# Two LayerNorm tiles instead of one per call in the attention loop of a fused attention and expert layer

## The chip, the cores and the metric

The kernel runs on the 8 cores of one Trainium2 chip. Each core works alone on half of one batch entry: 4096 tokens of 1024 channels. The cores exchange nothing. The metric is the device time in microseconds of the slowest core; lower is better.

## The reference

The layer is x + attention(LN(x)) + ffn(LN(x)). Attention covers every fourth token of a segment of 2048, so it has 512 tokens per segment, 16 heads of 64 channels and a causal mask. The feed-forward part has a shared expert and 8 routed ones (6 kept by rank), and covers all tokens.

```python
xn = _layernorm(x, axis=-1)
x = x + attn(xn, w_in, b_in, w_out, b_out) + ffn(xn, w1, w2, w3, ws1, ws2, ws3, wr)
# attn: only rows OFFSET::4 of each 2048-token segment; softmax over 512 keys, 16 heads
# ffn:  silu(x@ws1)*(x@ws2)@ws3 + sum_e w_e * (silu(x@w1[e])*(x@w2[e]))@w3[e]
```

## The kernel before, in words

A core has two segments (seg 0 and 1). A segment is split into four groups r = 0 to 3 of 512 tokens (every fourth token each), and a group into four tiles of 128 tokens. So there are 32 tiles, numbered here 0 to 31 in the order of the queue `lnq`; tiles 0 to 3 are group (0,0), 4 to 7 group (0,1), and so on. Attention is computed for r = 0 only, the feed-forward part for every group.

Each instruction is appended by `em` to a list of its engine, with the semaphore values that it waits for. The five engines work off their own lists in order, so the order of the calls below is the order on each engine.

**LayerNorm of a tile** has two steps.
- `ln_pre` (written P4 for tile 4): SyncE loads the tile into `XF` (two slots; the load waits until the normalisation two tiles earlier has read the slot). VectorE sums it (L316). ScalarE squares it (L318) and makes mean, squared mean (L322, L325). VectorE makes the variance (L328). ScalarE takes Ln and Exp (L332, L335). VectorE normalises into `xn_tm` (L338). ScalarE's square writes to the same slot of `xn_tm`, so it waits for the transposes two tiles earlier. The chain thus changes engine four times.
- `ln_tr` (written T4): TensorE transposes `xn_tm` eight times into a PSUM bank T0 or T1 (L356), VectorE copies the bank to `XN` (L365). `XN` holds two groups.

The banks T0 and T1 are taken in turn by a counter `trtile` that `ln_tr` and `attn_pair_out` share. The transposes of weight chunks use the same two banks, T0 for even and T1 for odd chunks, by a counter of their own.

**The pump.** `ln_pump` issues at most `maxtr` second steps and `maxpre` first steps, as far as two guards allow:

```python
def can_tr(i):
    if i >= len(lnq) or lnp["pre"] <= i + 1:
        return False
    seg, j = lnq[i]
    pu = prev_user[(seg, j // NQ)]
    return pu is None or pu in ffn_done
def can_pre(i):
    return i < len(lnq) and (i < 2 or lnp["tr"] >= i - 1)
...
while moved:   # T first, then P, until neither moves
    if ntr < maxtr and can_tr(lnp["tr"]): ln_tr(...)
    if npre < maxpre and can_pre(lnp["pre"]): ln_pre(...)
```

A tile is transposed only when the next one has had its first step issued; the first step runs at most two tiles ahead of the second; a group's place in `XN` must have been released by the feed-forward group that used it.

**Attention** (`attention(seg)`, L621 to L669) loops over eight head pairs hp = 0 to 7. One turn issues, in this order:
1. `attn_pair_out` of pair hp-2 (from hp = 2 on): four transposes of `OT` (L609), VectorE copies them to `OFM` (L616);
2. at hp = 4 `do_av(3)` and `v_batch(1)`, in seg 0 with four weight chunks ahead of it;
3. `qkv_pair(hp)`: in seg 0 first the weight chunks that this pair needs. A chunk is loaded into `WinNat` by GpSimd's queue, transposed on TensorE into T0 or T1 (L211) and copied by VectorE (L227); its load waits for the transposes of the chunk two earlier. Then Q (L433, L435) and K (L449, L452) on TensorE, which ScalarE copies out (L441, L457);
4. scores of key blocks 0 and 1 (L495, L498), `do_av(hp-1)` (L580, L583, then VectorE L591, L593), exps (L509, L514), scores of blocks 2 and 3 (L524, L527), exps (L539, L544), masks on VectorE (L559);
5. in seg 0 `wpump(2)`, which issues the next two items of the list of weights (two chunks at hp = 0, loads of expert weights at the later pairs);
6. `ln_pump()`, the call that is changed (L661).

The feed-forward groups call `ln_pump()` too, with its defaults of one and one. They are not touched. Attention of seg 1 has no weight chunks: all weights are in place.

Of the kernel before, what the change touches and what calls it, by code (L numbers as in the profile page):

```python
# [31 lines left out]
def build_nc():  # L32
# [20 lines left out]
    with ctx:  # L53
# [228 lines left out]
        def wpump(n=2):  # L282
            wensure(min(wptr[0] + n, len(witems)))
# [61 lines left out]
        def ln_tr(seg, j):  # L345
            r, q = j // NQ, j % NQ
            info = lninfo[(seg, j)]
            xsl = info["xsl"]
            state["trtile"] += 1
            tb = "T%d" % (state["trtile"] % 2)  # L350

            def mk_tr(xsl=xsl, tb=tb):
                def f(t):
                    ins = None
                    for ci in range(CI):
                        ins = t.transpose(bview[tb][:, ci, :],  # L356
                                          xn_tm[:, xsl, 128 * ci:128 * (ci + 1)], ident[:])
                    return ins
                return f
            ctr = em("tensor", mk_tr(), waits=[("sv", info["cxn"])] + bw(tb),  # L360
                     inc="sp")
            state["xntm_free"][xsl] = ("sp", ctr)
            rb = r % 2
            evw = [("sp", ctr)] + ([state["xnbuf_free"][rb]] if q == 0 else [])
            cev = em("vector", lambda v, rb=rb, q=q, tb=tb: v.tensor_copy(  # L365
                XN[:, rb, :, 128 * q:128 * (q + 1)], bview[tb][:, :, :]),
                waits=evw, inc="sv")
            bank[tb] = ("sv", cev)
            if q == NQ - 1:
                state["xn_ready"][(seg, r)] = cev  # L370
# [10 lines left out]
# [10 lines that stand above are left out]
        def ln_pump(maxtr=1, maxpre=1):  # L391
            ntr = npre = 0
            moved = True
            while moved:
                moved = False
                if ntr < maxtr and can_tr(lnp["tr"]):
                    ln_tr(*lnq[lnp["tr"]])
                    lnp["tr"] += 1
                    ntr += 1
                    moved = True  # L400
                if npre < maxpre and can_pre(lnp["pre"]):
                    ln_pre(*lnq[lnp["pre"]])
                    lnp["pre"] += 1
                    npre += 1
                    moved = True
# [160 lines left out]
        def av_head(seg, hp, pi, cmk):  # L566
            h = 2 * hp + pi
            obank = "Q" if pi == 0 else "K"
            ovw = oEv if pi == 0 else oOd
            vcol = 64 * h - 512 * (hp // 4)  # L570

            def mk_av(pi=pi, vcol=vcol, ovw=ovw):
                def f(t):
                    first = True
                    ins = None
                    for j in range(NQ):
                        for c in range(j + 1):
                            lt = pT[:, pi,
                                    PT_OFF[c] + 128 * (j - c):PT_OFF[c] + 128 * (j - c) + 128]
                            ins = t.matmul(ovw[:, j, 0:64], lt, Vsb[:, c, vcol:vcol + 64],  # L580
                                           start=first, stop=False)
                            first = False
                            ins = t.matmul(ovw[:, j, 64:65], lt, onescol[0:P, 0:1],  # L583
                                           start=False, stop=(j == NQ - 1 and c == j))
                    return ins
                return f
            cav = em("tensor", mk_av(),
                     waits=[("sv", cmk), state["vsb_ready"]] + bw(obank), inc="sp")
            state["pt_free"][pi] = ("sp", cav)

            crz = em("vector", lambda v, pi=pi, ovw=ovw: v.reciprocal(  # L591
                rz[:, pi, :], ovw[:, :, 64]), waits=[("sp", cav)], inc="sv")
            cno = em("vector", lambda v, pi=pi, ovw=ovw: v.tensor_tensor(  # L593
                OT[:, 0:NQ, 64 * pi:64 * pi + 64], ovw[:, :, 0:64],
                rz[:, pi, :, None].broadcast_to([P, NQ, 64]), op=ALU.mult),
                waits=[("sv", crz)] + ([state["ot_free"]] if pi == 0 else []),
                inc="sv")
            bank[obank] = ("sv", cno)
            return cno, cav

        def attn_pair_out(seg, hp, cno0, cno1):
            state["trtile"] += 1
            tb = "T%d" % (state["trtile"] % 2)

            def mk_tr(tb=tb):
                def f(t):
                    ins = None
                    for j in range(NQ):
                        ins = t.transpose(bview[tb][:, j, :], OT[:, j, :], ident[:])  # L609
                    return ins  # L610
                return f
            ctr = em("tensor", mk_tr(), waits=[("sv", cno0), ("sv", cno1)] + bw(tb),
                     inc="sp")
            state["ot_free"] = ("sp", ctr)
            evw = [("sp", ctr)] + ([state["ofm_free"]] if hp == 0 else [])
            cev = em("vector", lambda v, hp=hp, tb=tb: v.tensor_copy(  # L616
                OFM[:, hp, :], bview[tb][:, 0:NQ, :]), waits=evw, inc="sv")
            bank[tb] = ("sv", cev)
            return cev

        def attention(seg):  # L621
            pend_av = None
            pend_out = None
            last_ofm = None

            def do_av(hp, cmk_e, cmk_o):
                cne, cave = av_head(seg, hp, 0, cmk_e)
                cno, cavo = av_head(seg, hp, 1, cmk_o)
                if hp in (3, 7):
                    state["vsb_free"] = ("sp", cavo)  # L630
                    if hp == 7:
                        state["vsb_attn_done"] = ("sp", cavo)
                return cne, cno

            for hp in range(8):
                if pend_out is not None:
                    last_ofm = attn_pair_out(seg, *pend_out)
                    pend_out = None
                if hp == 4:
                    php, cmk_e, cmk_o = pend_av  # L640
                    cne, cno = do_av(php, cmk_e, cmk_o)
                    pend_out = (php, cne, cno)
                    pend_av = None
                    v_batch(seg, 1)
                eq, ek = qkv_pair(seg, hp)
                if hp == 0:
                    v_batch(seg, 0)
                cse_, cso_ = scores_c01(seg, hp, eq, ek)
                if pend_av is not None:
                    php, cmk_e, cmk_o = pend_av  # L650
                    cne, cno = do_av(php, cmk_e, cmk_o)
                    pend_out = (php, cne, cno)
                    pend_av = None
                cea, coa = exps_a(seg, hp, cse_, cso_, None)
                cse2, cso2 = scores_c23(seg, hp)
                ceb, cob = exps_b(seg, hp, cse2, cso2)
                cmk_e, cmk_o = masks(seg, hp, cea, coa, ceb, cob)
                pend_av = (hp, cmk_e, cmk_o)
                if seg == 0:
                    wpump(2)  # L660
                ln_pump()  # L661
            if pend_out is not None:
                last_ofm = attn_pair_out(seg, *pend_out)
            php, cmk_e, cmk_o = pend_av
            cne, cno = do_av(php, cmk_e, cmk_o)
            last_ofm = attn_pair_out(seg, php, cne, cno)
            state["ofm_ready"][seg] = last_ofm
# [256 lines left out]
        wensure(10)  # L924
        ensure_group(0, 0)
        attention(0)
        wensure(len(witems))
        for seg in range(NSEG):
            for r in range(NR):
                ensure_group(seg, r)  # L930
                ffn_group(seg, r)
                if seg == 0 and r == NR - 1:
                    flush_tail()
                    ensure_group(1, 0)
                    attention(1)
# [70 lines left out]
```

How the kernel before makes its waits and increments, by code:

```python
            def run(eng_obj, wt=wt, fn=fn, inc=inc, k=k):  # L139
                for s, v in wt:
                    eng_obj.wait_ge(S[s], v)
                ins = fn(eng_obj)
                if inc is not None:
                    ins.then_inc(S[inc], k)
```

## Time and profile before

| | us |
|---|---|
| two timed runs | 969.61 and 999.04, median 984.32 |
| the profiled execution, its own time | 973.35 |
| span of its slowest core (core 4), from the first to the last instruction | 971.7 |
| spans of the eight cores | 955.1 to 971.7 |
| attention of seg 0 on core 4, first Q matmul to the last transposes of `OT` | about 55 to 220 |
| attention of seg 1 on core 4 | about 554 to 665 |

The profiled execution's own time is 1.65 us more than the span of its slowest core. In the profile a line such as L338 is a line of the kernel. Busy time is summed per engine; a wait is given as "idle before, and who ended it". PE is TensorE's matmuls, DVE is VectorE, ACT is ScalarE, POOL is GpSimd and SP is SyncE.

### The profile page before, as it was taken

The page shows a single profiled execution, that of the slowest core. Times are in us where ns is not written, and L with a number is a line of the kernel's source. Part 1 is how long each engine was busy: PE and PEld are TensorE (multiplying, and loading weights), DVE is VectorE, ACT ScalarE, POOL GpSimd, SP SyncE. Part 2 cuts the span into 40 slices and gives each one's busy share as a digit, 9 for nine tenths or more (in the row PEclk, how much of TensorE's full clock was granted, in tenths as well). Part 3 has the DMA queues.
Part 4 walks back from the last instruction along what each step waited for, and adds up shares of the span by engine and source line. Part 5 has one row for each costly group of instructions (what it writes and reads, how often), then busy time and mean ns, then how long its engine had stood idle before and what let it go on. Part 6 is the DMA issues. An engine that isn't in the chain of part 4 may idle for free.

```text
span 971.7 us, 12064 instructions; the slowest of 8 cores (955.1 to 971.7 us)
## 1 busy us (share of the span) xinstructions
PE 736.2 (76%) x4126; PEld 337.5 (35%) x4192; DVE 272.2 (28%) x594; ACT 271.0 (28%) x464; POOL 94.1 (10%) x127
## 2 busy tenths in 40 slices
PE   1176646663999879958958977878999689598984
PEld 1123332333434333423423334334444233244432
DVE  3314231332330044035125024223220261232120
ACT  1223223230111163144144255332111441321111
POOL 3102021201001100200200200000002001101102
PEclk9996758675989978978979997878989799898988
DMA  5915565584003510720540630000015304502507
GB/s 100 160 45 90 84 85 69 61 136 65 1 1 76 141 45 1 168 92 1 122 116 22 129 110 22 1 2 1 1 25 117 112 8 82 136 0 42 133 3 171
DMA packets 48842, 67.40 MB, mean 69 GB/s; under 512 B 20880, under 2 KB 22928, under 8 KB 48784
## 3 DMA queue, kind: packets, MB, share of 16 engines
q0 software_dynamic: 34960, 33.06, 24.6%
q1 hardware_dynamic: 13824, 33.56, 10.3%
q8 instruction: 37, 0.61, 0.3%
q14 instruction: 21, 0.17, 0.1%
HBM read 66.11 MB, written 16.78 MB: 85 GB/s over the span
## 4 chain that ended last, share of the span: by engine, by line
PE 57%; DMA 16%; ACT 10%; DVE 8%; issue 8%; DVEq 0%; POOL 0%; ACTq 0%; SPq 0%; POOLq 0%
PE pA L821 10%; PE pB L821 8%; PE pK L874 6%; PE pQ L874 6%; PE pA L433 5%; PE pA L742 5%; DMA WinNat<-x 4%; DMA XF<-x 4%; PE pA L449 3%; PE pB L742 3%; DMA out<-osb 2%; PE ptT L211 2%; DVE st_s L316 2%; DMA WinNat<-w_in 2%; DMA osb<-x 2%
## 5 line engine op out<-in xcount | busy, mean ns | idle before, releaser
L821 PE MATMUL pA<-XN,W 128*128 128x512 bf16 x497 | 125.5, 407 | 57.2 <-ACT s1e L835 56.1
L821 PE MATMUL pB<-XN,W 128*128 128x512 bf16 x501 | 114.3, 379 | 0.6
L821 PEld LDWEIGHTS pA<-XN,W 128*128 128x128 bf16 x512 | 51.1, 103 | 123.1 <-issue 76.1
L897 POOL DMA_DIRECT2D osb<-x x32 | 27.2, 850 | 615.3 <-ACT osb L892 612.4
L211 PE MATMUL ptT<-ident,WinNat 128*128 128x128 bf16 x256 | 29.8, 299 | 66.0 <-DMA WinNat<-w_in 25.9
L821 PEld LDWEIGHTS pB<-XN,W 128*128 128x128 bf16 x512 | 50.1, 98 | 60.4
L874 PE MATMUL pQ<-W,HP 128*128 128x512 bf16 x252 | 63.7, 395 | 0.2
L874 PE MATMUL pK<-W,HP 128*128 128x512 bf16 x254 | 60.4, 379 | 0.2
L835 ACT ACTIVATE s1e<-pA 128x1024 bf16<-128x1024 f32 x32 | 32.7, 1023 | 85.3 <-PE pA L821 85.1
L316 DVE TENSOR_REDUCE st_s<-XF 128x1 f32<-128x1024 f32 x32 | 38.8, 1212 | 57.2 <-DMA XF<-x 57.2
L318 ACT ACTIVATE xn_tm<-XF 128x1024 bf16<-128x1024 f32 x32 | 33.7, 1052 | 74.5 <-DMA XF<-x 64.7
L433 PE MATMUL pA<-XN,Wqk 128*128 128x512 bf16 x116 | 44.3, 549 | 8.2 <-DVE Wqk L227 5.4
L211 PEld LDWEIGHTS ptT<-ident,WinNat 128*128 128x128 bf16 x256 | 24.3, 136 | 70.9 <-issue 70.9
L559 DVE TENSOR_TENSOR pT<-pT,utri 128x128 bf16<-128x128 bf16 x128 | 20.2, 221 | 94.7 <-ACT pT L539 93.0
L839 DVE TENSOR_TENSOR HP<-s1e,pB 128x1024 bf16<-128x1024 bf16 x32 | 39.0, 1218 | 27.7 <-PE pB L821 19.2
L742 PE MATMUL pA<-XN,Ws 128*128 128x512 bf16 x120 | 44.2, 544 | 1.5 <-issue 0.7
L804 DVE TENSOR_TENSOR HP<-HP,pQ 128x512 bf16<-128x512 bf16 x32 | 22.0, 688 | 80.7 <-PE pQ L796 79.3
L785 DVE COPY gT<-pQ 8x512 bf16<-8x512 bf16 x8 | 3.3, 410 | 141.9 <-PE pQ L779 141.9
L356 PE MATMUL ptT<-ident,xn_tm 128*128 128x128 bf16 x256 | 23.5, 245 | 21.6 <-DVE xn_tm L338 21.6
L338 DVE TENSOR_SCALAR xn_tm<-XF,st_m,st_r 128x1024 bf16<-128x1024 f32 x32 | 26.0, 813 | 45.9 <-ACT st_r L335 45.9
L874 PEld LDWEIGHTS pQ<-W,HP 128*128 128x128 bf16 x256 | 25.8, 101 | 32.8 <-issue 4.5
L874 PEld LDWEIGHTS pK<-W,HP 128*128 128x128 bf16 x256 | 25.0, 98 | 30.5 <-issue 0.6
(146 smaller groups left out, 923.8 us busy)
## 6 DMA issues: line engine op xcount, KB each, us to landing
XF<-x SPq DMA_DIRECT2D x32, 512.0 KB, 4.5
osb<-x POOLq DMA_DIRECT2D x32, 256.0 KB, 4.5
out<-osb SPq DMA_DIRECT2D x32, 256.0 KB, 4.8
WinNat<-x POOLq DMA_DIRECT2D x32, 256.0 KB, 5.4
out<-WinNat SPq DMA_DIRECT2D x32, 256.0 KB, 3.2
WinNat<-w_in POOLq DMA_DIRECT2D x24, 256.0 KB, 4.9
W<-w POOLq DMA_DIRECT2D x16, 256.0 KB, 6.7
W<-w POOLq DMA_DIRECT2D x1, 2048.0 KB, 19.7
```

What stands on the lines that cost most here:

```text
L211: ins = t.transpose(bview[tb][:, ci, :], WinNat[:, sl, 128 * ci:128 * (ci + 1)], ident[:])
L316: crs = em("vector", lambda v, seg=seg, j=j, gslot=gslot: v.reduce_sum(st_s[:, seg, j:j + 1], XF[:, gslot, :], axis=AX), waits=ldw, inc="sv")
L318: csq = em("scalar", lambda s, seg=seg, j=j, gslot=gslot, xsl=xsl: s.activation(out=xn_tm[:, xsl, :], in_=XF[:, gslot, :], func=AF.Square, ...
L338: cxn = em("vector", lambda v, seg=seg, j=j, gslot=gslot, xsl=xsl: v.tensor_scalar(out=xn_tm[:, xsl, :], in0=XF[:, gslot, :], scalar1=st_m ...
L433: t.matmul(pA[:, 0, :], Wqk[:, ci, 128 * hp:128 * (hp + 1)], XN[:, 0, ci, :], start=(ci == 0), stop=False)
L449: t.matmul(pA[:, 1, :], Wqk[:, ci, 1024 + 128 * hp:1024 + 128 * (hp + 1)], XN[:, 0, ci, :], start=(ci == 0), stop=False)
L742: ins = t.matmul(bview[bn], Wsx[:, ci, 128 * k:128 * (k + 1)], XN[:, rb, ci, :], start=(ci == 0), stop=(ci == CI - 1))
L821: ins = t.matmul(bview[bn], Wx[:, e, ci, :], XN[:, rb, ci, :], start=(ci == 0), stop=(ci == CI - 1))
L835: cse = em("scalar", lambda s: s.activation(out=s1e[:, :, :], in_=pA[:, :, :], func=AF.Silu), waits=[("sp", cw10), ("sp", cw11), last_chp2 ...
L839: cu = em("vector", lambda v, e0=e0: v.tensor_tensor(HP[:, e0:e0 + 2, :], s1e[:, :, :], pB[:, :, :], op=ALU.mult), waits=[("sa", cse), ("s ...
L874: ins = t.matmul(bview[bn], lt, rh, start=(i == 0), stop=(i == len(ops) - 1))
L897: em("gpsimd", lambda g, seg=seg, r=r, q=q, Hh=Hh, dst=dst: g.dma_start(out=dst, in_=xv[seg, r, q][:, 512 * Hh:512 * (Hh + 1)], accum_op=A ...
```

## The change

The call at the end of a turn of the attention loop may issue up to two second steps and two first steps:

```diff
@@ -658,7 +658,7 @@
                 pend_av = (hp, cmk_e, cmk_o)
                 if seg == 0:
                     wpump(2)
-                ln_pump()
+                ln_pump(maxtr=2, maxpre=2)
             if pend_out is not None:
                 last_ofm = attn_pair_out(seg, *pend_out)
             php, cmk_e, cmk_o = pend_av
```

## Rows read from the trace of the kernel before

**Rows 1.** The page's busy times and granted TensorE clock over 40 slices.

```profile
PE 736.2 (76%) x4126; PEld 337.5 (35%) x4192; DVE 272.2 (28%) x594; ACT 271.0 (28%) x464; POOL 94.1 (10%) x127
...
PEclk9996758675989978978979997878989799898988
```

**Rows 2.** Waits of TensorE, 50 to 240 us: us in total, times, longest.

```profile
PE ptT L211 <- DVE OFM L616: 21.4, 6, 5.6
```

**Rows 3.** VectorE, timeline, seg 0 around the end of hp=0.

```profile
75.82 1.21 DVE L316 TENSOR_REDUCE st_s<-XF 128x1 f32<-128x1024 f32 x1
78.58 0.81 DVE L338 TENSOR_SCALAR xn_tm<-XF,st_m,st_r 128x1024 bf16<-128x1024 f32 x1 [0.70 <-ACT st_r L335]
84.78 0.18 DVE L591 RECIPROCAL rz<-pQ 128x4 f32<-128x4 f32 x1 [5.39 <-PE pQ L583]
```

**Rows 4.** TensorE, timeline, seg 0: Q of hp=1.

```profile
75.77 3.57 PE L433 MATMUL pA<-XN,Wqk 128*128 128x512 bf16 x8 [1.22 <-DVE Wqk L227]
```

**Rows 5.** VectorE, timeline, end of hp=1: P and T ahead of OFM.

```profile
88.59 1.21 DVE L316 TENSOR_REDUCE st_s<-XF 128x1 f32<-128x1024 f32 x1
...
92.68 0.41 DVE L616 COPY OFM<-ptT 128x512 bf16<-128x512 bf16 x1
```

**Rows 6.** VectorE, timeline, ends of hp=4, hp=5 and hp=6 in seg 0.

```profile
166.00 1.22 DVE L316 TENSOR_REDUCE st_s<-XF 128x1 f32<-128x1024 f32 x1
...
170.38 0.41 DVE L616 COPY OFM<-ptT 128x512 bf16<-128x512 bf16 x1
...
185.37 1.21 DVE L316 TENSOR_REDUCE st_s<-XF 128x1 f32<-128x1024 f32 x1
...
188.86 0.42 DVE L616 COPY OFM<-ptT 128x512 bf16<-128x512 bf16 x1
...
202.50 0.42 DVE L616 COPY OFM<-ptT 128x512 bf16<-128x512 bf16 x1
```

**Rows 7.** TensorE, timeline, seg 0: weight chunks after hp=3, hp=5, hp=6.

```profile
131.28 1.87 PE L211 MATMUL ptT<-ident,WinNat 128*128 128x128 bf16 x16 [3.10 <-DVE rz L591]
...
189.43 1.01 PE L211 MATMUL ptT<-ident,WinNat 128*128 128x128 bf16 x8 [4.07 <-DVE OFM L616]
...
203.06 1.86 PE L211 MATMUL ptT<-ident,WinNat 128*128 128x128 bf16 x16 [1.44 <-DVE OFM L616]
205.72 0.63 PE L433 MATMUL pA<-XN,Wqk 128*128 128x512 bf16 x1 [0.79 <-DVE Wqk L227]
```

**Rows 8.** VectorE, timeline, seg 1, end of hp=0.

```profile
573.46 1.21 DVE L316 TENSOR_REDUCE st_s<-XF 128x1 f32<-128x1024 f32 x1
...
576.22 0.81 DVE L338 TENSOR_SCALAR xn_tm<-XF,st_m,st_r 128x1024 bf16<-128x1024 f32 x1 [0.70 <-ACT st_r L335]
580.13 0.18 DVE L591 RECIPROCAL rz<-pQ 128x4 f32<-128x4 f32 x1 [3.10 <-PE pQ L583]
```

**Rows 9.** ScalarE, timeline, seg 1: Q and K copied out, hp=1 and hp=2.

```profile
576.02 0.58 ACT L441 ACTIVATE Q<-pA 128x512 bf16<-128x512 f32 x1
577.88 0.60 ACT L457 ACTIVATE K<-pA 128x512 bf16<-128x512 f32 x1 [1.28 <-PE pA L452]
...
587.11 0.58 ACT L441 ACTIVATE Q<-pA 128x512 bf16<-128x512 f32 x1
589.23 0.60 ACT L457 ACTIVATE K<-pA 128x512 bf16<-128x512 f32 x1 [1.54 <-PE pA L452]
```

**Rows 10.** TensorE, timeline, seg 1: a turn end with LayerNorm (593) and one without (637).

```profile
593.59 0.37 PE L524 MATMUL pB<-Q,K 64*128 64x256 bf16 x1 [0.44 <-ACT pT L514]
...
595.67 3.19 PE L433 MATMUL pA<-XN,Wqk 128*128 128x512 bf16 x7 [0.22 <-issue]
...
637.04 0.37 PE L524 MATMUL pB<-Q,K 64*128 64x256 bf16 x1 [0.59 <-ACT pT L514]
...
638.27 1.06 PE L433 MATMUL pA<-XN,Wqk 128*128 128x512 bf16 x2 [0.22 <-ACT pT L544]
```

**Rows 11.** Loads of a LayerNorm tile, all 32.

```profile
DMA to landing us min/median/max: 3.3/4.5/10.9
```

## The prediction, made before the changed kernel ran

> **What bounds the kernel now.** I read the page first. TensorE is busy 76% of the span, VectorE and ScalarE 28% each [rows 1]. So the end is set by TensorE and by what TensorE waits for, and the question for this change is where LayerNorm stands in TensorE's way. The granted clock says where TensorE is thin: its digits are lowest in the 4th to 9th slice of 24 us, which is attention of segment 0.
>
> Then the waits of TensorE in that stretch. The largest is for weight chunks, six times, 21.4 us in all, and it is ended by VectorE's copy of `OFM` [rows 2]. A chunk's transposes need bank T0 or T1, the bank is freed by that copy, and the copy stands on VectorE behind the LayerNorm step that the pump issued at the end of the turn before. The timelines show it: at the end of hp=1 the tile's reduction starts at 88.59 and `OFM` follows at 92.68, 4.09 us later [rows 5]. At hp=5, where only a P is issued, it is 188.86 - 185.37 = 3.49 us, and at hp=6, without LayerNorm, the chunks wait only 1.44 us [rows 6, 7]. So in segment 0 each tile's chain of engine changes lies bare on the path. In segment 1 there are no chunks, Q and K of the next pair do not wait for VectorE, and the same chain lies beside them: ScalarE takes Q out at 576.02, just after the chain's last step [rows 8, 9].
>
> **What the change issues.** The calls follow from the guards. Segment 0 enters attention with tiles 0 to 3 done. Before: hp=0 P4; hp=1 P5 T4; hp=2 P6 T5; hp=3 P7 T6; hp=4 P8 T7; hp=5 P9; then tile 8 is held back, as its place in `XN` is in use. After: hp=0 P4 P5 T4; hp=1 P6 T5 P7 T6; hp=2 P8 T7 P9; nothing later. Segment 1 enters with T19 and P21 done. Before: hp=0 to 3 one pair each (T20 P22 to T23 P25). After: hp=0 T20 P22 T21 P23; hp=1 T22 P24 T23 P25; nothing later. Both ways leave attention with the same tiles done (T7, P9 and T23, P25), so every feed-forward call is what it was. No instruction is added or removed; ten steps of work move two or three pairs earlier. They lay one to a turn and now lie two to a turn.
>
> **Segment 0, turn by turn.**
> - End of hp=0: P4 cost nothing before. It ran on VectorE while TensorE did Q and K of hp=1, and VectorE was idle for 5.39 us before the next `rz` [rows 3]. P5 (3.49 us) fits there. But T4 is now issued on TensorE ahead of Q of hp=1 and waits for P4's normalisation, which ends at 78.58 + 0.81 = 79.39. Eight transposes take 1.01 us (the same shape at L211 [rows 7]), so Q starts at about 80.4 in place of 75.77 [rows 4]: **+4.6**. Behind T4 on TensorE stand Q, K, the scores and AV of the pair, and all wait with it. This is the one new wait.
> - End of hp=1: one P and T become two, in series on VectorE, all ahead of `OFM`: **+4.1** [rows 5]. T6 on TensorE waits for P6, but P7 holds `OFM` longer.
> - End of hp=2: P8 T7 P9 in place of P6 T5: one P more, **+3.5** [rows 6].
> - End of hp=3: P7 T6 are gone. `trtile` now gives `OT`'s transposes the other bank, so the first chunk no longer needs `OFM` at all; it needs the AV matmuls to be out of the way. TensorE's idle time ahead of it, 3.10 us, goes: **-3.1** [rows 7].
> - End of hp=4: P8 T7 gone, reduction 166.00 to `OFM` 170.38: **-4.4** [rows 6].
> - End of hp=5: P9 gone: **-3.5** [rows 6]. Next late there, as at hp=6, is the wait from the masks over `OFM` to the chunks [rows 7].
>
> Sum: 12.2 given, 11.0 got back, **+1.2**. What was serial stays serial; the change loses because T4 stands in front of its own first step and gains nothing for it. The bounds of the T4 term: 0 if Q of hp=1 had been as late anyway, 4.6 as worked out; the row of Q at 75.77 says that it was not late, so I take 4.6.
>
> **Segment 1.** Here ScalarE's order decides. Q's copy is issued behind the whole chain of the pump. Before, it started 576.02 - 573.46 = 2.56 us after the reduction [rows 8, 9], and Q's last matmul was just done. With a second P behind the first (and T21's copy between), the second reduction starts 4.09 us after the first, at 577.55, and Q's copy at 580.1; K's follows 0.6 us later, at 580.7, against 577.88: **+2.8**. The scores of hp=1 wait for K, and exps, masks and the pair's end behind them. VectorE's own 3.10 us of idle time ahead of `rz` [rows 8] hides nearly all of its part, since AV moves too. At hp=2 the same: Q at 587.11 + 4.09 = 591.2, K at 591.8 against 589.23: **+2.6**. In return the turn ends of hp=2 and hp=3 lose their transposes. From the last score matmuls to Q it is 595.67 - 593.59 = 2.08 us with LayerNorm and 638.27 - 637.04 = 1.23 us without [rows 10]: **-0.9** at hp=2. At hp=3 AV waits for the masks anyway; I take half of it, **-0.5**. Sum: **+4.0**. Bounds: below, 1.4 us less than nothing, if ScalarE's copies were not held up at all; above 5.4, if nothing came back.
>
> Both together: 973.35 + 1.2 + 4.0 = **978.5 us**, against the profiled execution. The two runs shown lie at 969.61 and 999.04; the profiled one is near the lower, and the median of the two, 984.32, is not a time that any run had. A change of +0.5% is well within the 2% that a measurement of this kernel can about tell from no change.
>
> **The clock.** Waits grow at three turns and shrink at three. In segment 0 the Q matmuls run at the low level, 1.2 GHz, after long waits and short ones: 3.57 us for eight after 1.22 us of idle time [rows 4], 0.63 us for the first one of hp=7 after 0.79 us, with 1.44 us before the chunks [rows 7]. So I count no change. The Trainium skill says (TensorE: Matmul & The Clock Gate, section "Why this matters for your kernels") that idle gaps between bursts of matmuls put the array back to half its clock. By that rule doubling three waits costs and the shortened ones pay; the trace agrees that matmuls after a wait run low, but it shows no turn of segment 0 whose Q was spared. By the rule the sum would lie in the rival next below.
>
> **The rivals.**
> 1. The clock is lost where waits grow. Q of eight matmuls costs 3.57 us low [rows 4]; at the upper level (half of that) it would be 1.8. If the low level spreads from Q over K and the rest of each of five lengthened turns, that is up to 1.8 x 5 = 9 us, more likely half: 983. For it: two of the digits in segment 0 are already 5 and 6 [rows 1]. Against: the waits are there already.
> 2. The clock is kept where waits shrink: three turns of segment 0 and two of segment 1 win up to 1.8 us each, some 6 us in all: 972.5, no change seen. For it: the digits of attention go from 5 to 9, so both levels occur within it [rows 1]; against, the row of 0.63 us after a short wait.
> 3. Slower by over 2%: the second load of a pair comes late. SyncE's load of a tile waits for the slot until the tile two before is normalised, and two steps now stand close together. Five second steps (P5, P7, P9, P23, P25) would each wait up to a landing, 4.5 us median, 10.9 at most [rows 11]. At the median for all it is 978.5 + 22.5 = 1001. It decides only if slot release and reduction are less than a landing apart; I reckon about 10 us for P25 (P23's normalisation at about 581, its reduction at about 591.6) and more in segment 0, as a whole turn lies between. Unlikely.
> 4. The chains of two tiles overlap. P and P are in different slots, and ScalarE's square of the second may run beside the first's VectorE steps. If a second chain cost only its VectorE work (1.21 + 0.81 us and the copy) and not its waits, each double turn is 1.5 us cheaper, five of them: 971. VectorE's order, which issues the second reduction behind the first normalisation, speaks against it.
>
> **Chances.** Forecast 0.60 (978.5, own range 975 to 982). rival 1 0.14, rival 2 0.10, rival 3 0.04, rival 4 0.06; the rest, 0.06, is divided between unforeseen gains and losses. Executions differ by 4 us without any change (969.61 against 973.35), and one of the shown ones is far above; rival 1 reaches 988. So the range is 967 to 991. Over 2% faster (below about 954) needs something that none of these has: 0.04. Over 2% slower (above 993): rival 3 and part of rival 1, 0.08. Within 2%: 0.88.
>
> **What would show it.** In the profile after: no L316, L338 or L356 after hp=2 of segment 0's attention and after hp=1 of segment 1's. L356 before Q of hp=1 with an idle time of about 4.5 us ended by DVE L338. Reduction to `OFM` about 8.2 us at the end of hp=1, 7.6 at hp=2, and nothing at hp=3 to 5. In segment 1, L441 of hp=1 and hp=2 right behind L335 of the second tile, and K's copies 2.6 to 2.8 us later in their turn. Both attentions together about 5 us longer, the feed-forward groups as they were. I am wrong if the heads without LayerNorm get shorter by more than 4.4 us each, if the doubled chains take less than 7 us, or if an XF load is named as the releaser of a reduction in either attention.

## The result: slower by half a per cent

| | before | after |
|---|---|---|
| median of the runs, us | 973.25 (30 runs) | 977.88 (31 runs) |
| ratio, 95% interval | | 1.0054 (1.0037 to 1.0071) |
| span of the slowest core in the profile, us | 971.7 | 976.4 |
| mean granted TensorE clock of that core | 0.861 | 0.861 |

The ratio is that of the means of 27 and 30 of these runs, without the four that lie far above the others. 1.0054 x 973.25 is a change of +5.3 us (the two medians differ by 4.6); the sum of the prediction's terms was +5.2. The kernel got slower, and the interval leaves out 1, although the change is far below 2%. The slowest core is now core 2, where it was core 4 before, so the parts of the span are compared over all eight cores.

From the first Q matmul to the last transposes of `OT`, the attention of segment 0 took 161.4 us before and 162.7 after (medians of the eight cores of the profiled executions), and that of segment 1 took 111.5 and 116.6. The three parts around them, whose instructions are the same, add to 680.7 and 680.3 us. So the loss is in the two attentions, +1.3 and +5.1 us, and most of it in segment 1. That this is 6.4 and not 5.3 lies within what single executions do: the last part alone, behind segment 1's attention, has medians between 291.5 and 295.4 us in the ten kernels of this document, with the same instructions.

**The page after** (span, granted clock over 40 slices):

```profile
span 976.4 us, 12063 instructions; the slowest of 8 cores (964.7 to 976.4 us)
PEclk9996668775989988979978987787999799798998
```

The clock's string differs from [rows 1] in single digits, up and down. Its mean is the same.

**The waits of TensorE between 50 and 240 us.** First core 2 before the change, then core 2 after (columns as in [rows 2]):

```profile
PE ptT L211 <- DVE OFM L616: 20.8, 6, 5.0
PE ptT L356 <- DVE xn_tm L338: 4.4, 1, 4.4
```

```profile
PE ptT L211 <- DVE OFM L616: 16.1, 6, 8.2
PE ptT L356 <- DVE xn_tm L338: 13.1, 3, 4.5
```

A reader who looks only at the first line sees a gain of 4.7 us. It is more than given back in the second: TensorE's wait for a tile's normalisation went from one (4.4 us, ahead of attention) to three, 8.7 us more. Much of the wait did not go away, it changed its name.

**TensorE in segment 0, after.** T4, Q of hp=1, the second T at the end of hp=1 (T6), and the chunks at the ends of hp=1, 2, 3 and 4, the first two with the Q behind them:

```profile
79.72 1.01 PE L356 MATMUL ptT<-ident,xn_tm 128*128 128x128 bf16 x8 [4.48 <-DVE xn_tm L338]
80.53 3.47 PE L433 MATMUL pA<-XN,Wqk 128*128 128x512 bf16 x8
...
96.50 1.01 PE L356 MATMUL ptT<-ident,xn_tm 128*128 128x128 bf16 x8 [4.17 <-DVE xn_tm L338]
...
101.52 1.86 PE L211 MATMUL ptT<-ident,WinNat 128*128 128x128 bf16 x16 [3.58 <-DVE OFM L616]
104.17 3.19 PE L433 MATMUL pA<-XN,Wqk 128*128 128x512 bf16 x7 [0.79 <-DVE Wqk L227]
...
124.43 1.86 PE L211 MATMUL ptT<-ident,WinNat 128*128 128x128 bf16 x16 [8.16 <-DVE OFM L616]
127.08 2.17 PE L433 MATMUL pA<-XN,Wqk 128*128 128x512 bf16 x7 [0.79 <-DVE Wqk L227]
...
139.31 1.87 PE L211 MATMUL ptT<-ident,WinNat 128*128 128x128 bf16 x16
...
173.62 1.86 PE L211 MATMUL ptT<-ident,WinNat 128*128 128x128 bf16 x16 [1.65 <-DVE OFM L616]
```

T4 waits 4.48 us for L338, with Q right behind it: that is the new wait of the prediction. At the end of hp=2 the chunks wait 8.16 us. At the end of hp=3 they wait for nothing; before it was 3.10 us [rows 7].

**VectorE at the ends of hp=1 and hp=4, after** (answers to [rows 5, 6]):

```profile
92.78 1.22 DVE L316 TENSOR_REDUCE st_s<-XF 128x1 f32<-128x1024 f32 x1
...
96.87 1.21 DVE L316 TENSOR_REDUCE st_s<-XF 128x1 f32<-128x1024 f32 x1
...
100.96 0.41 DVE L616 COPY OFM<-ptT 128x512 bf16<-128x512 bf16 x1
...
171.84 1.30 DVE L559 TENSOR_TENSOR pT<-pT,utri 128x128 bf16<-128x128 bf16 x8 [8.56 <-ACT pT L539]
173.06 0.42 DVE L616 COPY OFM<-ptT 128x512 bf16<-128x512 bf16 x1
```

From reduction to reduction it is 4.09 us, and again 4.09 us to `OFM`: the second chain costs as much as the first, and nothing overlaps. At hp=4 `OFM` follows the masks at once.

**ScalarE in segment 1, after** (answers to [rows 9]): the last step of the second chain, then Q and K, at hp=1 and hp=2.

```profile
579.49 0.20 ACT L335 ACTIVATE st_r<-st_v 128x1 f32<-128x1 f32 x1
579.59 0.58 ACT L441 ACTIVATE Q<-pA 128x512 bf16<-128x512 f32 x1
580.07 0.59 ACT L457 ACTIVATE K<-pA 128x512 bf16<-128x512 f32 x1
...
593.43 0.20 ACT L335 ACTIVATE st_r<-st_v 128x1 f32<-128x1 f32 x1
593.54 0.58 ACT L441 ACTIVATE Q<-pA 128x512 bf16<-128x512 f32 x1
594.02 0.59 ACT L457 ACTIVATE K<-pA 128x512 bf16<-128x512 f32 x1
```

Neither copy has an idle time before it. At hp=1 the last of K's matmuls had ended at 577.8, 2.3 us before K's copy began; Q and K stand in ScalarE's line behind LayerNorm. TensorE's wait for K's copy (L495, between 554 and 670 us) grew accordingly:

```profile
PE pA L495 <- ACT K L457: 10.2, 7, 3.1
```

On core 2 before it was 6.7 us in the same seven waits, at most 1.0. The 3.5 us more and the 1.4 us of one turn that is explained further down make up nearly all of the 5.1.

**The turns over all cores.** For each core I took from the timelines the time from the end of a pair's last mask to the first Q matmul of the next pair (segment 0), and the median of the eight cores:

| before pair | 1 | 2 | 3 | 4 | 5 | 6 | 7 |
|---|---|---|---|---|---|---|---|
| before, us | 1.06 | 6.84 | 6.84 | 27.86 | 7.14 | 4.98 | 2.75 |
| after, us | 5.64 | 10.93 | 10.34 | 25.06 | 2.76 | 1.40 | 2.76 |
| difference | +4.6 | +4.1 | +3.5 | -2.8 | -4.4 | -3.6 | 0 |
| predicted | +4.6 | +4.1 | +3.5 | -3.1 | -4.4 | -3.5 | 0 |

Each of the six terms comes out within 0.3 us. Their sum is +1.4. For segment 1 the same table is not of use, since Q no longer follows the masks; there I took the distance from one copy of Q to the next (hp=0 to 1, 1 to 2 and so on, median of eight cores): before 19.51, 11.47, 12.41, 20.87; after 23.45, 13.95, 9.83, 22.25. Up to the copy of hp=4 that is 64.3 and 69.5 us: +5.2. The three distances behind it together add 0.5, and the stretch from the copy of hp=7 to the end of attention gives 0.6 back.

### The profile page after: what moved, and what is told of

The parts are those of the page before. It is cut to its first block, busy times and chain, and to the rows that moved or that the text cites. A ratio compares the mean times of both kernels' runs of the same rounds, so it can differ in the third digit from the quotient of the medians.

```text
span 976.4 us, 12063 instructions; the slowest of 8 cores (964.7 to 976.4 us)
## 1 busy us (share of the span) xinstructions
PE 734.3 (75%) x4125; PEld 337.4 (35%) x4192; DVE 273.0 (28%) x594; ACT 270.7 (28%) x464; POOL 94.2 (10%) x127
## 4 chain that ended last, share of the span: by engine, by line
PE 55%; DMA 16%; ACT 10%; DVE 8%; issue 8%; POOL 0%; DVEq 0%; ACTq 0%; SPq 0%; POOLq 0%
PE pA L821 9%; PE pB L821 8%; PE pK L874 6%; PE pQ L874 6%; PE pA L742 4%; DMA WinNat<-x 4%; PE pA L433 4%; DMA XF<-x 4%; PE pB L742 3%; PE pA L449 3%; DVE st_s L316 3%; DMA out<-osb 2%; DMA WinNat<-w_in 2%; PE ptT L211 2%; DMA osb<-x 2%
## 5 line engine op out<-in xcount | busy, mean ns | idle before, releaser
L316 DVE TENSOR_REDUCE st_s<-XF 128x1 f32<-128x1024 f32 x32 | 38.7, 1211 | 60.1 <-DMA XF<-x 60.1
L742 PE MATMUL pA<-XN,Ws 128*128 128x512 bf16 x120 | 42.0, 522 | 1.6 <-issue 0.7
L338 DVE TENSOR_SCALAR xn_tm<-XF,st_m,st_r 128x1024 bf16<-128x1024 f32 x32 | 26.0, 812 | 45.6 <-ACT st_r L335 45.6
```

What stands on the lines that cost most here:

```text
L316: crs = em("vector", lambda v, seg=seg, j=j, gslot=gslot: v.reduce_sum(st_s[:, seg, j:j + 1], XF[:, gslot, :], axis=AX), waits=ldw, inc="sv")
L338: cxn = em("vector", lambda v, seg=seg, j=j, gslot=gslot, xsl=xsl: v.tensor_scalar(out=xn_tm[:, xsl, :], in0=XF[:, gslot, :], scalar1=st_m ...
L742: ins = t.matmul(bview[bn], Wsx[:, ci, 128 * k:128 * (k + 1)], XN[:, rb, ci, :], start=(ci == 0), stop=(ci == CI - 1))
```

## The experiments

All ratios are against the kernel before, on the same chip, with a 95% interval. Stretches and distances are medians of the eight cores in the profiled execution.

**Each segment alone.**

```diff
-                ln_pump()
+                if seg == 0:
+                    ln_pump(maxtr=2, maxpre=2)
+                else:
+                    ln_pump()
```

> Two tiles per call in segment 0's attention only, segment 1 as before. My theory: the turn ends of segment 0 change by +4.6, +4.1, +3.5, -3.1, -4.4 and -3.5 us, in sum +1.2 us, a ratio of 1.001 (974.5 us for 973.3). Rival (all of the loss is in segment 0, the clock lost in the longer waits): +5 us, ratio 1.005. Rival (the second chain in a turn comes cheaper): below 1.000.

Measured: 1.0019 (0.9992 to 1.0046). The stretches from masks to Q are 5.64, 10.94, 10.34, 25.26, 2.75, 1.40: the change's own. TensorE's waits are the new ones, on another core (core 4):

```profile
PE ptT L211 <- DVE OFM L616: 16.1, 6, 8.2
PE ptT L356 <- DVE xn_tm L338: 13.7, 3, 5.1
```

The interval holds 1.001 and leaves out the first rival's 1.005, narrowly. It does not leave out a ratio just below 1.000, the second rival; the stretches do, since the doubled chains cost their full 4.1 and 3.5 us in them. The attention of segment 0 took 163.4 us, against 161.4 before.

The other way round, with `seg == 1` in the condition:

> Two tiles per call in segment 1's attention only, segment 0 as before. My theory: ScalarE copies K out 2.8 and 2.6 us later at hp=1 and hp=2, 0.9 and 0.5 us come back, so +4.0 us, ratio 1.004; the trace of the changed kernel reads nearer to +5 us, so up to 1.005. Together with the run of segment 0 alone it should give the whole change's 1.0054. Rival (segment 1 hides it, the loss is in segment 0): 1.000.

Measured: 1.0029 (1.0004 to 1.0055), a small rise, clear of 1. Segment 0 has its old stretches (1.07, 6.85, 6.85, 27.33, 7.14, 4.98). 1.0019 x 1.0029 is 1.0048 for the whole change's 1.0054. By the central values both segments lose and segment 1 loses more, but the loss of segment 0 alone is not clear of 1.000 and the intervals are wider than the difference between the two, so the split rests on the turns in the traces. From Q's copy at hp=0 to that of hp=4 the medians sum to 69.2 us, as in the changed kernel.

**T4 out of Q's way.**

```diff
-                ln_pump()
+                if seg == 0:
+                    ln_pump(maxtr=(0 if hp == 0 else 2), maxpre=2)
+                else:
+                    ln_pump()
```

> Segment 0 only: two tiles per call, but the call of hp=0 issues its two first steps and no T4; T4 comes at hp=1 with T5. Calls: hp=0 P4 P5; hp=1 T4 P6 T5 P7; hp=2 T6 P8 T7 P9. My theory: TensorE's wait of 4.5 us ahead of Q of hp=1 is gone (-4.6 us against the run of segment 0 alone), hp=2's end has one more T copied by VectorE (+0.6 us): 4.0 us less than that run, which is -2.8 us against before, ratio 0.997. Rival (Q of hp=1 would have been late anyway, T4 only shows the wait): same as the run of segment 0 alone, 1.001.

Measured: 0.9984 (0.995 to 1.0018) against 1.0019 for segment 0 alone. The intervals of the two overlap, so the time alone leaves it open; the stretch from masks to Q of hp=1 does not: 1.07 us in place of 5.64. So T4's wait was the whole of that term. The +0.6 us of a further T came at the end of hp=2 (10.93 against 10.34), as expected. Not expected was that the end of hp=1 fell from 10.94 to 9.59: with one T fewer ahead of it, the counter `trtile` gives the first chunk a bank that is freed by VectorE's copy of a tile (L365), ahead of the second chain; only the second chunk still waits for `OFM`. Something was paid for it which the expectation had left out, and ScalarE's timeline shows it:

```profile
78.91 0.20 ACT L335 ACTIVATE st_r<-st_v 128x1 f32<-128x1 f32 x1
79.02 0.58 ACT L441 ACTIVATE Q<-pA 128x512 bf16<-128x512 f32 x1
79.49 0.59 ACT L457 ACTIVATE K<-pA 128x512 bf16<-128x512 f32 x1
```

With Q early again, its copy stands behind P5's steps: from Q's first matmul to its copy it is 6.10 us against 4.20 before. It is segment 1's mechanism, met in segment 0.

**Transposes moved, chains not.**

```diff
-                ln_pump()
+                if seg == 1:
+                    ln_pump(maxtr=2, maxpre=1)
+                else:
+                    ln_pump()
```

> Segment 1 only: up to two second steps but one first step per call: hp=0 T20 P22 T21, hp=1 P23 T22, hp=2 P24 T23, hp=3 P25. The chains stay one to a turn, only transposes move. My theory (ScalarE's order behind a doubled chain is the cost): nearly nothing, -0.5 to +1.0 us, ratio 0.9995 to 1.001. Rival (the added transposes on TensorE are the cost): half or more of what segment 1 alone costs, +2 us or more, 1.002 or above.

Measured: 0.9995 (0.9969 to 1.0021). The interval just reaches the rival's 1.002, so the trace has to decide. ScalarE at hp=2 of segment 1, with the idle time before K's copy that the changed kernel has no more (at hp=1 it is 1.55 us too):

```profile
582.47 0.20 ACT L335 ACTIVATE st_r<-st_v 128x1 f32<-128x1 f32 x1
582.75 0.60 ACT L441 ACTIVATE Q<-pA 128x512 bf16<-128x512 f32 x1
584.90 0.60 ACT L457 ACTIVATE K<-pA 128x512 bf16<-128x512 f32 x1 [1.55 <-PE pA L452]
```

K waits for TensorE again. So it is the doubled chain on ScalarE and not the added transposes that costs the time at hp=1 and 2. By the distances between copies of Q (20.03, 11.17, 12.35) the first three turns are at +0.2 us against before; the fourth, 22.24, is 1.4 us longer, as in the changed kernel. The expectation had nothing for it. The whole attention of segment 1 took 113.1 us, against 111.5 before and 116.5 with the chains doubled as well: of the 5.0 us, 1.6 come with the moved transposes and 3.4 with the doubled chains. The 1.4 us are taken up below.

**Only the part of the change that has free room.**

```diff
-                ln_pump()
+                if seg == 0 and hp == 0:
+                    ln_pump(maxtr=0, maxpre=2)
+                else:
+                    ln_pump()
```

> Default pump everywhere but at hp=0 of segment 0, which issues P4 and P5 (no T4). Then hp=1 T4 P6, hp=2 T5 P7, hp=3 T6 P8, hp=4 T7 P9, and nothing at hp=5. My theory: VectorE's free stretch before the first rz takes P5; the 3.5 us of P9 at the end of hp=5 go, and Q's copy at hp=1 comes some 1.7 us later behind P5's steps on ScalarE: -1.8 us net, ratio 0.998. Rival (no free stretch): 1.000 or above.

Measured: 0.9976 (0.9953 to 0.9999). VectorE at the end of hp=0:

```profile
75.15 1.21 DVE L316 TENSOR_REDUCE st_s<-XF 128x1 f32<-128x1024 f32 x1
...
78.64 1.22 DVE L316 TENSOR_REDUCE st_s<-XF 128x1 f32<-128x1024 f32 x1
...
83.93 0.18 DVE L591 RECIPROCAL rz<-pQ 128x4 f32<-128x4 f32 x1 [1.71 <-PE pQ L583]
```

Two chains, and VectorE still waits 1.71 us for TensorE: the room was there. The interval ends just below the rival's 1.000, and the trace supports it: the end of hp=5 falls from 4.98 to 1.49 us, and Q's copy at hp=1 comes 1.9 us later, near the 1.7 of the expectation. Moving a P pays only if it goes from where it is bare (an engine on the path waits for it) to where it is covered (nothing waits for it); the tested change moved P6 to P9 from one bare place to another.

**The chain behind the chunks.** If in segment 0 every bare P is on the path because it stands ahead of `OFM`, the place should be changed and not the number:

```diff
             wensure(max(widx[hp], widx[8 + hp]) + 1)
+            if seg == 0 and hp > 0:
+                ln_pump(maxtr=0, maxpre=1)
 ...
-                ln_pump()
+                ln_pump(maxtr=1, maxpre=(0 if seg == 0 else 1))
```

> One tile per turn as before, but in segment 0 the first step P is issued after the weight chunks of the next pair, ahead of Q, and T stays at the turn's end. My theory (in segment 0 the chain of P ahead of OFM is what the chunks wait for): the stretches from the masks' end to Q shrink by about 3.5 us at hp=2, 3, 5 and 6 each and 3 us at hp=4: -16 us, ratio 0.984. Rival (the chain only shows beside another bound, such as the chunk loads, or delays Q's copy on ScalarE by as much): less than -5 us, above 0.995.

Measured: 0.981 (0.9773 to 0.9847), which holds the expected 0.984 and leaves out the rival. The stretches before pairs 2 to 6 are 1.49, 3.10, 25.34, 3.06 and 3.11 us, 17.6 us less in sum than before, and the attention of segment 0 took 144.9 us in place of 161.4.

Then T as well, behind K's matmuls in segment 0:

```diff
                 eq, ek = qkv_pair(seg, hp)
+                if seg == 0:
+                    ln_pump(maxtr=1, maxpre=0)
 ...
-                ln_pump(maxtr=1, maxpre=(0 if seg == 0 else 1))
+                if seg == 1:
+                    ln_pump()
```

> As the run with P late, and in segment 0 T is issued after K's matmuls, where TensorE waits 0.95 us for ScalarE's copy of K. My theory: T's copy by VectorE (0.6 us) leaves the way of OFM too, four times: -18 us against before, ratio 0.981. Rival (T delays the scores by its full 1.0 us): as the run with P late alone or up to 2 us slower than it.

Measured: 0.9792 (0.9738 to 0.9846). Stretches 1.48, 1.48, 23.89, 1.43, 1.49. By the ratio it can't be told from the run before; by the stretches another 6.3 us went, where the expectation had 2: not only T's copy but its transposes too (1.0 us of TensorE) left the way. Q's batches take some back (from Q's first matmul to its copy at hp=5 and 6 3.98 and 3.88 us, against 3.64 and 3.00), and the attention of segment 0 as a whole took 140.2 us, 4.7 less. VectorE shows the new order (in this kernel and the next L316 and L338 keep their numbers, lines behind the insertion are two higher):

```profile
101.86 0.42 DVE L618 COPY OFM<-ptT 128x512 bf16<-128x512 bf16 x1
102.19 0.68 DVE L227 COPY Wqk<-ptT 128x1024 bf16<-128x1024 bf16 x1
103.54 0.69 DVE L227 COPY Wqk<-ptT 128x1024 bf16<-128x1024 bf16 x1 [0.67 <-PE ptT L211]
104.15 1.21 DVE L316 TENSOR_REDUCE st_s<-XF 128x1 f32<-128x1024 f32 x1
```

And T behind K in both segments:

```diff
-                if seg == 0:
-                    ln_pump(maxtr=1, maxpre=0)
+                ln_pump(maxtr=1, maxpre=0)
 ...
                 if seg == 1:
-                    ln_pump()
+                    ln_pump(maxtr=0, maxpre=1)
```

> As the run before, and in segment 1 too T is issued after K's matmuls, P at the turn's end. My theory: three of four turns of segment 1 lose 0.9 us of TensorE time between the last scores and Q: -20 us against before, ratio 0.979. Rival (clock levels and ScalarE's copy of Q behind the chain hide it): no better than the run without it.

Measured: 0.9788 (0.9759 to 0.9816), median 950.07 us against 971.22. It is the fastest version of the study, 2.1% faster than the kernel before and 2.6% faster than the changed one (0.9788 / 1.0054 = 0.9735). The step from the run before is not resolved, and the 0.979 agrees with the expectation although its reason does not: the expectation had 2 us from segment 1, and the attention of segment 1 took 111.1 us against 110.7 in the run before. The distance from Q's copy at hp=2 to that at hp=3 fell from 12.34 to 11.22 us, but the next one, which has the batch of V in it, rose from 20.98 to 22.09. So the gain against the kernel before is segment 0's. TensorE in segment 0, T behind K and the scores after it:

```profile
108.39 0.62 PE L356 MATMUL ptT<-ident,xn_tm 128*128 128x128 bf16 x8
109.41 0.37 PE L497 MATMUL pA<-Q,K 64*128 64x512 bf16 x1 [0.40 <-ACT K L459]
```

The scores still wait for K's copy, so T cost them nothing. In the waits of 50 to 240 us (core 4) the copy of `OFM`, once the first line with 21.4 us, is down to the fourth:

```profile
PE ptT L211 <- DVE OFM L618: 5.5, 6, 1.5
```

## What the prediction had right, and the steps that failed

Two steps failed: the term for the end of hp=3 in segment 1 (-0.5 forecast, +1.4 measured), which rested on counting no change for the clock, and the base on which the forecast as a time was put. The places of the new waits and the costs of the chains were right. By its steps:

- **What the change issues.** Right: T4 ahead of Q at the end of hp=0, two tiles in one turn at hp=1 and hp=2 (P8 T7 P9), none after; the feed-forward part is untouched. By the prediction's own lists fifteen steps move, by one to three pairs, and not ten by two or three; no term hangs on it.
- **Segment 0, six terms.** Each right within 0.3 us in the stretches. The run without T4 showed that the 4.6 us are T4's wait. What the sum left out is how long Q's own matmuls take at the granted clock: from Q's first matmul to its copy it was, at hp=1 to 7 before, 4.20, 2.98, 3.99, 2.30, 3.38, 3.50, 2.98 us and after 3.84, 4.05, 2.92, 2.30, 3.90, 3.76, 3.12: up and down by 1.1, +0.6 in sum.
- **Segment 1.** The chain ahead of Q's copy and K's behind it: right in place and, at 4.09 us more from reduction to reduction, in its working. Between the copies of Q of hp=0 and hp=3 three distances give 43.4 before and 47.2 after, +3.8, against 2.8 + 2.6 - 0.9 = 4.5.
- **The term that failed** is "At hp=3 AV waits for the masks anyway; I take half of it, -0.5". T23 did leave that turn, yet the turn got longer, by 1.4 us (20.87 to 22.25). T's leaving brought only 0.2 us (from the last score matmul to V's first 2.83 and 2.65 us, medians), and from V's first matmul to Q's it took 8.86 us before and 10.47 after. The batch of V got slower. First the kernel before (core 4), then the changed one (core 2):

```profile
609.57 1.76 PE L473 MATMUL pA<-Wv,XN 128*128 128x512 bf16 x7 [0.24 <-issue]
```

```profile
613.09 3.19 PE L473 MATMUL pA<-Wv,XN 128*128 128x512 bf16 x7 [0.24 <-issue]
```

The same seven matmuls take 1.76 us before and 3.19 after. The stretches of the timeline around them (us from and to, PE, PEld, DVE, ACT, POOL busy, granted clock, DMA share, GB/s), before and after:

```profile
606.00:609.50 3.50, 3.29 (x54) 3.13 (x56) 2.91 (x10) 2.13 (x4) 0.00 (x0) 0.55 0.02 5
609.50:615.00 5.50, 5.43 (x23) 2.12 (x23) 2.42 (x8) 2.01 (x6) 0.00 (x0) 0.98 0.00 0
```

```profile
612.00:616.00 4.00, 3.76 (x29) 1.72 (x27) 1.22 (x4) 0.00 (x0) 0.00 (x0) 0.50 0.02 4
```

  Before, the granted clock was low from about 606.3 to 609.7 us, while TensorE did T23, `OT`'s transposes and AV; V found the upper level. After, it was low from about 609.4 to 616.2 us, from the last scores through `OT`'s transposes and AV to the end of V's first batch. All ten kernels agree. Where T's eight transposes stand at the end of hp=3 (the kernel before, segment 0 alone, T4 out of the way, the free room, P late, and P and T late in segment 0), V's first seven or eight matmuls took 1.68 to 2.26 us on 41 of 48 cores and 2.83 to 3.58 on the other seven. Where they do not (the changed kernel, segment 1 alone, transposes moved, and T behind K in both segments) they took 2.85 to 3.58 us on all 32. Segment 1's attention starts up to some 20 us earlier in the kernels with P late, and even there V's time goes with where T stands, so T's place is the cause and not a shift of the whole turn in time. V starts only 0.2 us earlier behind the scores without T, which leaves TensorE's work on T as the likely reason; other work in T's place was not tried.
- **The clock at no change.** The failure of that term is the clock's, which the prediction had put at nothing ("So I count no change"), and the reading behind it was too narrow. The row of 0.63 us at hp=7 [rows 7] is one matmul at the edge of what was read; the whole batch, and that of hp=4, are in the trace of the kernel before (core 4):

```profile
156.46 1.67 PE L433 MATMUL pA<-XN,Wqk 128*128 128x512 bf16 x7 [1.03 <-DVE Wqk L227]
...
205.72 2.29 PE L433 MATMUL pA<-XN,Wqk 128*128 128x512 bf16 x7 [0.79 <-DVE Wqk L227]
```

  Seven matmuls take 3.19 us at the low level, so the batch of hp=4 ran at the upper one: both levels occurred in segment 0, and what moves in front of a batch can change which one it gets. In segment 1's attention the granted clock was low for 38 us before and 46 after (medians); Q's and K's matmuls took as long in sum as before (39.8 and 39.5 us), so it cost what V's batch shows.
- **The base.** The forecast of 978.5 is 973.35, the profiled execution, plus 5.2, and says slower by 0.5%. Beside the median of the two runs in the table, 984.32, the same time reads as a fall of 0.6%, and the kernel rose by 0.5%. The two bases lay 11 us apart, twice the effect, and the direction hung on the choice between them, which stood in one sentence. Thirty runs put the kernel before at 973.25, so the profiled execution was the base that held.
- **The sum.** +5.2 was forecast, +5.3 measured by the runs and +6.4 read from the two attentions of the profiled executions, with one error of -0.5 for +1.4 in it and others that went the other way. That the forecast meets the runs' figure so closely is partly luck.
- **The rivals.** The clock lost for good (1) and kept (2): the mean is 0.861 both times, and in segment 0 Q's batches move by 1.1 us either way. The weaker form of 1 is what happened at the V batch. (The chance of over 2% slower was given in part to rival 1, which by its own sum reaches only 988, below 993.) Late loads (3): on core 2 none of the waits of ScalarE and VectorE in either attention ends with an `XF` load; the landings are nearly as in [rows 11]:

```profile
DMA to landing us min/median/max: 3.3/4.6/11.4
```

  Overlapping chains (4): 4.09 and 4.09 us, no overlap. The Trainium skill's rule on idle gaps (TensorE: Matmul & The Clock Gate, "Why this matters for your kernels") spoke for a loss by doubled waits. The trace agrees that the array is at the low level in such a wait: the granted clock was 0.50 throughout the 8.16 us, and throughout the 3.58 us of the turn before. But the 8.16 us were followed by Q at 2.17 us for seven matmuls, and the 3.58 us by Q at 3.19. So here the length of the last gap does not tell how long a batch runs low.

## What to carry to other kernels

A helper that issues "background" work into in-order engines has two settings, how much and where, and the second is worth more: here doubling the amount cost 0.5%, and moving the same work from ahead of the copies that TensorE waits for to behind them gained 2.1%, of which the first steps of segment 0 alone gave 1.9%. Before work is pulled forward, write down for each engine what is queued behind it at the new place, and whether the old place was bare or covered. Count the granted clock as a term of its own where the work that moves stood in front of a long batch of matmuls. A step that needs the end of a chain across four engine changes must not be issued in front of independent TensorE work in the same breath.

## What the runs showed that was not expected

- Taking eight transposes (1.0 us) away from a turn made it 1.4 us longer, because the low clock level then fell on 512-column matmuls: 3.19 in place of 1.76 us for seven. It was so on all eight cores after (distance of Q's copies at least 21.9 us) and on one of eight before (22.5 against 20.7 to 20.9 on the others), and the fastest kernel pays it too (22.09 us).
- The chain of a LayerNorm tile is very regular where VectorE goes on to the next work at once: 3.49 us without and 4.09 us with the copy of another tile's transposes, in both segments and in all ten kernels. The one exception is the end of hp=4 in segment 0, 4.38 us [rows 6].
- A wait that falls in the list of releasers can have moved to another name: `OFM` fell by 4.7 us on core 2 while the tile's normalisation rose by 8.7.
